# Two layers of windowed attention with relative positions: the token order inside the attention becomes column by column within each pair of image rows

## The reference, cut to what matters

```python
attn = einsum('bqd,bkd->bqk', q * scale, k)
rel_h = einsum('bhwc,hkc->bhwk', qr, Rh)      # table chosen by the query's row h
rel_w = einsum('bhwc,wkc->bhwk', qr, Rw)      # table chosen by the query's column w
attn = attn.reshape(B*nh, H, W, H, W) + rel_h[:, :, :, :, None] + rel_w[:, :, :, None, :]
out = softmax(attn.reshape(B*nh, HW, HW)) @ v
x = x + out @ proj_w.T + proj_b               # once per layer
```

## Time and profile before

| | us |
|---|---|
| median of 3 runs (lowest, highest) | 2332.41 (2329.14, 2334.24) |
| the profiled execution | 2339.97 |
| its span, first to last instruction | 2338.2 |
| TensorE, VectorE, ScalarE, GpSimd busy | 2094.7, 1653.4, 1621.4, 714.4 |
| mean granted TensorE clock in the span | 0.978 of full speed |

### The profile page before, as it was taken

One profiled execution on the slowest core, in us unless ns is written; L12 is line 12 of the kernel. 1 busy time (PEld: TensorE's weight loads), 2 busy tenths in 40 slices (PEclk: granted clock), 3 DMA queues, 4 the chain that ended last, 5 costly groups with the idle time before them and its releaser, 6 DMA issues.

```text
span 2338.2 us, 73485 instructions
## 1 busy us (share of the span) xinstructions
PE 2094.7 (90%) x27904; PEld 1595.9 (68%) x27904; DVE 1653.4 (71%) x3923; ACT 1621.4 (69%) x3713; POOL 714.4 (31%) x1796
## 2 busy tenths in 40 slices
PE   1899999999999989999999999899989999999998
PEld 1677676776767767667667766677766766777765
DVE  5677777667767677777677777677767777777675
ACT  0577777677767667767676777677767776777675
POOL 1233323333333233333233333233223333333230
PEclk9899999999999999999999999999999999999999
DMA  1333434333434333433333443344334343334331
GB/s 47 84 94 95 104 91 105 91 92 91 103 93 97 90 94 93 101 93 93 91 98 91 94 103 96 88 96 100 91 91 102 94 100 93 94 93 103 91 92 47
DMA packets 170550, 216.34 MB, mean 93 GB/s; under 512 B 29783, under 2 KB 138072, under 8 KB 170202
## 3 DMA queue, kind: packets, MB, share of 16 engines
q1 hardware_dynamic: 170202, 211.64, 37.7%
HBM read 117.00 MB, written 57.80 MB: 75 GB/s over the span
## 4 chain that ended last, share of the span: by engine, by line
PE 39%; DMA 33%; SPq 14%; DVE 6%; issue 4%; ACT 3%; POOL 1%; POOLq 0%; ACTq 0%; DVEq 0%
PE ps_m L412 18%; DMA q_st<-mrow 17%; DMA k_dram<-qk_hl 10%; PE ps_sc L538 7%; PE ps_max L525 6%; SPq L375 6%; DMA q_dram<-qk_hl 6%; DVE qk_hl L734 4%; PE ps_o L557 3%; SPq L382 3%; ACT qk_hl L598 2%; SPq L341 2%; SPq L387 2%; PE ps_m L501 2%; DVE rel_hl L776 1%
## 5 line engine op out<-in xcount | busy, mean ns | idle before, releaser
L722 DVE TENSOR_REDUCE mx<-ps_max 98x2 f32<-98x392 f32 x1536 | 819.4, 562 | 232.6 <-PE ps_max L525 215.5
L586 ACT ACTIVATE probs<-ps_sc 98x392 f32<-98x392 f32 x1536 | 714.5, 497 | 232.3 <-PE ps_sc L538 198.2
L525 PE MATMUL ps_max<-k_st,q_st 124*98 124x196 f16 x3072 | 548.9, 261 | 82.4 <-DVE mx L722 82.1
L538 PE MATMUL ps_sc<-q_st,k_st 125*98 125x196 f16 x3072 | 523.3, 252 | 95.6 <-DMA q_st<-mrow 94.1
L776 DVE TENSOR_TENSOR rel_hl<-ps_m,rel_hi 64x504 f16<-64x504 f32 (+1 forms) x768 | 431.4, 562 | 162.0 <-ACT rel_hi L643 152.9
L525 PEld LDWEIGHTS ps_max<-k_st,q_st 124*98 124x98 f16 x3072 | 295.0, 126 | 296.4 <-issue 198.0
L538 PEld LDWEIGHTS ps_sc<-q_st,k_st 125*98 125x98 f16 x3072 | 320.9, 126 | 123.1 <-DMA q_st<-mrow 120.4
L557 PE MATMUL ps_o<-probs,v_st 98*32 98x196 f32 x6144 | 389.6, 340 | 0.5 <-ACT o_sb L578 0.5
L634 ACT ACTIVATE rel_hi<-ps_m,is_lo 64x504 f16<-64x504 f32 (+1 forms) x384 | 223.9, 583 | 189.1 <-PE ps_m L471 185.7
L471 PE MATMUL ps_m<-q_st,rel_st 64*32 64x84 f16 x7168 | 341.6, 266 | 4.8 <-DVE rel_hl L776 4.5
L809 POOL TENSOR_TENSOR msq<-mv 96x2 f32<-96x2 f32 x128 | 24.4, 191 | 1007.1 <-DVE mv L748 1007.1
(11 more groups left out here) (72 smaller groups left out, 3293.8 us busy)
## 6 DMA issues: line engine op xcount, KB each, us to landing
q_st<-q_dram SPq DMA_DIRECT2D x128, 294.0 KB, 3.8
k_st<-k_dram SPq DMA_DIRECT2D x256, 147.0 KB, 3.9
q_dram<-qk_hl SPq DMA_DIRECT2D x128, 147.0 KB, 2.6
k_dram<-qk_hl SPq DMA_DIRECT2D x128, 147.0 KB, 2.7
q_st<-rel_hl SPq DMA_DIRECT2D x256, 73.5 KB
q_st<-rel_hl SPq DMA_DIRECT2D x256, 64.3 KB
xa<-in_x SPq DMA_DIRECT2D x64, 147.0 KB
xd<-in_x SPq DMA_DIRECT2D x64, 147.0 KB
```

Of the source, the lines that this page charges most:

```text
L525: last = nc.tensor.matmul(ps_max[head % 2][0:HT, h * TOK:h * TOK + TOK], q_st[u.r][0:R_MAX, head, h, :], k_st[u.r][0:R_MAX, head, :], star ...
L538: last = nc.tensor.matmul(ps_sc[head % 2][0:HT, kt * TOK:kt * TOK + TOK], k_st[u.r][0:STACK, head, kt * HT:kt * HT + HT], q_st[u.r][0:STAC ...
L586: nc.scalar.activation(probs[head][:, :, :], ps_sc[head % 2][0:HT, 0:2 * TOK].rearrange("p (k t) -> p k t", k=2), ACT.Exp, scale=1.0 / (QS ...
L722: nc.vector.reduce_max(mx[u.r % 2][:, head, :], ps_max[head % 2][0:HT, 0:2 * TOK].rearrange("p (q k) -> p q k", q=2), axis=AX.X).then_inc( ...
```

## The change

Tokens are ordered column by column within each pair of rows: token number = 28 x (row / 2) + 2 x column + (row mod 2), the integer quotient taken. The tokens are put into this order where ScalarE copies `xT` out of PSUM, and put back where it copies `o_sb`. The one-hot rows are put into it once, by a new VectorE copy into `oh_f16`, from which the 48 copies are now made (f16 to f16). In the rel matmuls a row's 14 queries now lie 4 bytes apart and its results 8 bytes apart; a column's queries lie in seven pairs per head, the two of a pair next to each other both in `q_st` and in the bank, the pairs 56 bytes apart in `q_st` and 48 in the bank (16 in `rel2`). The evacuations of a bank keep their number and their sizes; the column ones write runs of 12 elements (4 in `rel2`) instead of 6 (2). No slot, bank, buffer or DMA changes.

```diff
         oh_raw = sb("oh_raw", [128, TOK])
+        oh_f16 = sb("oh_f16", [128, TOK], F16)
...
-            by_col = (dst[64:128, :, :].rearrange("p h (a b) -> p (h a) b", a=SIDE)[:, :, a0:a0 + n],
-                      ps[64:128, 0:n * HH * SIDE].rearrange("p (x b) -> p x b", b=n))
+            by_col = (dst[64:128, :, :].rearrange("p h (k x) -> p (h k) x", k=HALF)[:, :, 2 * a0:2 * (a0 + n)],
+                      ps[64:128, 0:n * HH * SIDE].rearrange("p (x y) -> p x y", y=2 * n))
...
                                 if axis == 0:
-                                    to = to.rearrange("p (h a b) -> p h a b", h=HH, a=rows)[:, :, i, :]
+                                    to = to.rearrange("p (h k b r) -> p h k r b", h=HH, r=2, b=SIDE)[:, :, i // 2, i % 2, :]
+                                    q = q.rearrange("p h (k b r) -> p h k r b", r=2, b=SIDE)[:, :, a // 2, a % 2, :]
                                 else:
-                                    to = to.rearrange("p (x b) -> p x b", b=rows)[:, :, i]
-                                last = nc.tensor.matmul(
-                                    to, rel_st[:, lay, axis, w:w + RW],
-                                    q[:, :, a * SIDE:a * SIDE + SIDE] if axis == 0 else q[:, :, a::SIDE],
-                                    start=True, stop=True)
+                                    to = to.rearrange("p (x b r) -> p x b r", b=rows, r=2)[:, :, i, :]
+                                    q = q.rearrange("p h (k b r) -> p (h k) b r", r=2, b=SIDE)[:, :, a, :]
+                                last = nc.tensor.matmul(to, rel_st[:, lay, axis, w:w + RW], q, start=True, stop=True)
...
-                            nc.scalar.copy(o_sb[u.r % 2][:, g, :], ps_o[:, 0:TOK]).then_inc(s_o, 1)
+                            nc.scalar.copy(o_sb[u.r % 2][:, g, :].rearrange("p (k r b) -> p k r b", r=2, b=SIDE),
+                                           ps_o[:, 0:TOK].rearrange("p (k b r) -> p k r b", r=2, b=SIDE))\
+                              .then_inc(s_o, 1)
...
-                        nc.scalar.copy(xT[u.r % 2][:, :, :],
-                                       ps_m[BANK["xT"]][0:CC, 0:2 * TOK].rearrange("p (c t) -> p c t", c=2))\
+                        nc.scalar.copy(xT[u.r % 2][:, :, :].rearrange("p c (k b r) -> p (c k) b r", r=2, b=SIDE),
+                                       ps_m[BANK["xT"]][0:CC, 0:2 * TOK]
+                                       .rearrange("p (k r b) -> p k b r", r=2, b=SIDE))\
                           .then_inc(s_xT, 1)
...
             dve.wait_ge(s_const, 16 * 8)
+            nc.vector.tensor_copy(oh_f16[R_REL:STACK, :].rearrange("p (k b r) -> p k r b", r=2, b=SIDE),
+                                  oh_raw[R_REL:STACK, :].rearrange("p (k r b) -> p k r b", r=2, b=SIDE)).then_inc(s_oh, 1)
+            dve.wait_ge(s_oh, 1)
             for i in range(UNROLL):
                 for head in range(HEADS):
-                    nc.vector.tensor_copy(k_st[i][R_REL:STACK, head, :], oh_raw[R_REL:STACK, :])
+                    nc.vector.tensor_copy(k_st[i][R_REL:STACK, head, :], oh_f16[R_REL:STACK, :])
```

More of the change, by code:

```diff
@@ L161, in attention_kernel @@
         s_wlo = sem("s_wlo")
+        s_oh = sem("s_oh")
         s_setup = sem("s_setup")
```

## The result

The changed kernel takes 2392.88 us (median of 4 runs, 2390.59 to 2403.28), the kernel before 2330.77 (4 runs, 2325.98 to 2334.24). The ratio is 1.0277, 95% interval 1.0241 to 1.0313: 62 us slower.

What follows compares the result with a forecast made beforehand. It took a ring through the DRAM round trip and second mrow DMA to bound the kernel. Savings of 7 us and a net 41 us from added clock falls made +34, so 2366 us, range 2322 to 2396.

Steps and rivals of the forecast that it cites:

- the likeliest case: Shorter rel bursts lengthen TensorE's wait before head 6, so the clock falls more often; 2345 to 2390, more falls 0.63.
- The picture of the ring: Loop: qk cast, DRAM round trip, second mrow DMA, head 6, next cast; about 11 us outside TensorE, 6.2 on it.
- Column step: One step of column matmuls in a rel burst: from 0.158 us to 0.079 with pairs, half as many separate accesses.
- Burst lengths: Rel matmul bursts on TensorE: rel0 and rel1 lose 0.40 us each, rel2 0.08; first and second from 1.10 to about 0.7.
- The two waits: TensorE's waits for the maxima (takes up rel1's 0.40 us) and before head 6 (0.48 longer; 94 to about 150 us total).
- Falls: Granted clock dropping to its lower level around head 6: 17 units before, 45 forecast, 28 more, from shares by wait length.
- The place of the falls: Falls were forecast around head 6; rel1's 0.40 us was to vanish in the wait for the maxima.
- The price of a fall: Each clock fall around head 6 lengthens TensorE's slots 10 to 3 from 6.22 to 7.80 us, 1.6 us.
- The sum: Gain of 7 us and net loss of 41 from clock falls: +34, put on the median 2332.41, gives 2366.
- no change: Rel bursts stay as long because separate-word writes set their pace; only the start's -2: 2330; within the bound 0.19.
- faster: Shorter bursts without more clock falls before head 6: -7, and -5 more, 2323 to 2326; faster 0.18 in all.
- Slower by more: Column and row matmuls both at row pace: waits grow 0.72 us, 39 more falls, 2384, or 2400 if longer; chance 0.2.

Runs made afterwards that it cites:

- e7: Kernel before, with rel column matmuls reading runs of 14 and writing one run (wrong column terms), for shorter bursts; 2540.34 us, ratio 1.083.
- e1: Changed kernel plus 8 matmuls with overwritten results before head 6's wait for the second mrow DMA; 2342.43 us, ratio 1.0007 to the kernel before.
- e3: Changed kernel with SyncE issuing the second mrow DMA before it waits for q and k's round trip (three slot numbers); 2165.62 us.
- e4: Kernel before, with SyncE issuing the second mrow DMA before it waits for q and k's round trip (three slot numbers); 2199.61 us.
- e8: Changed kernel with the second mrow DMA issued earlier and 8 overwritten matmuls in slot 8, before the wait for the maxima; 2117.89 us.
- e10: Kernel before, with the second mrow DMA issued earlier and 8 overwritten matmuls in slot 8; 2197.58 us, ratio 0.9402.
- e2: Changed kernel plus overwritten matmuls, 8 before head 6's wait and 6 in slot 8 before the wait for the maxima; 2332.78 us, ratio 0.9986.
- e5: Kernel before, with single-element reads in rel0's column matmuls and single-word writes in rel1's, reading and writing kept apart (wrong terms); 2412.29 us, one run.
- e6: Kernel before, with paired reads in rel0's column matmuls and paired writes in rel1's, kept apart (wrong terms); 2545.64 us, one run.

## Why the prediction was right, and where its sizes were off

The direction, the sign's cause and the range (2322 to 2396) held; the time was 2366 against 2392.88, so the loss was 62 us where 34 was said. The time is only 3 us inside the range, and above the 2390 to which the likeliest case alone was said to reach.

The ring of each unit can be cut in two at the first `qk` cast. Means over the 123 units that have both parts, counted from the traces (us; the clock is "low" in a unit where it stood at the lower level for some of TensorE's part):

| | head 6 to `qk` cast (TensorE) | `qk` cast to head 6 (the rest) | units with the clock low in TensorE's part, and that part in them |
|---|---|---|---|
| before | 6.48 | 11.12 | 17, 8.13 |
| changed | 6.94 | 11.13 | 48, 8.06 |
| e7 | 7.49 | 11.39 | 99, 7.80 |
| e1 | 6.32 | 11.32 | 8, 7.95 |

Where the clock stayed, TensorE's part takes 6.21 or 6.22 us in all four. So the loss is in TensorE's part, 56 us over these units, and the rest of the ring has not changed.

- **The picture of the ring**: right. DMA and its issue are still some four tenths of the chain, and e3 and e4 show the ring by opening it. The sign I had named against it, units at full clock shorter by 0.4 us, did not come: head 6 to head 6 takes 17.32 us before and 17.18 after (means of 101 and 65 of these units), and their scatter does not tell 0.14 from nothing.
- **Column step**: 0.079 forecast, 0.076 measured (0.379 us from the first to the last of a burst, a fifth of it). My reason, a cost per separate access, fits the reads of singles and pairs; I allowed row matmuls 0.079 at most, and they pace at 0.067.
- **Burst lengths**: the first mis-sized term. I counted five steps (0.40 us) and 0.08 for rel2, but the last matmul of a burst is shorter as well. 1.10 went to 0.63 and 0.47 to 0.33, together 0.61 us and not 0.48. With the ring open and the clock held, the mean unit is 0.59 us shorter (15.77 in e8, 16.36 in e10).
- **The two waits**: 51 us more for the maxima, as rel1's 0.40 us x 128 = 51 said; 50 us more before head 6, 61 said. The 13 units with a fall in the middle all reach head 6 without a wait.
- **Evacuations, permuted copies**: no change, as taken. **Start**: -2.3 us, -2 said. The 4 us of the units without a wait can't be seen: the rest of the ring is 1 us longer over the 123 units. Such units were miscounted, too: 24 have no wait over 0.15 us, not 13, and 128 less the 105 waits of the earlier trace rows is already 23.
- **Falls**: 45 near head 6 forecast, 35 came, and 13 came in the middle, behind the wait for the maxima. The profile before had none there. That 48 is near 45 is luck in part: two errors meet. Near head 6 the share of long waits with a fall was too high, as it stood on 8 waits: of the 38 waits over 1.6 us in the changed kernel 26 were followed by a fall, where 7 of 8 were before (6 of 21 between 1.2 and 1.6, 3 of 34 between 0.7 and 1.2, none of 34 below).
- **The place of the falls**: the step that is wrong in kind is the one that has rel1's 0.40 us go "into the standstill behind the maxima" at no cost, though that standstill grew from 0.63 to 1.04 us. A fall there can take TensorE's slack and more (21.6 us for the unit above), and all 13 run on into TensorE's part of the next unit, which takes 8.20 us in them. 17 falls hold 72 us at the lower level before, 4.2 us each, and 48 hold 270 after, 5.6 each, because those of the middle are so long.
- **The price of a fall**: 1.6 us forecast, 1.9 before and 1.8 after (8.13 and 8.06 against 6.22). I had priced one fall from the earlier trace rows, 7.80 us; the 17 of the same trace would have given 1.9. e1 says the same: 8 units with the clock low for 48 take 75 us off TensorE's part, 1.9 each, while the rest of the ring grows by 23 us with the fillers.
- **The sum**: the two profiled executions differ by 51 us (2390.59 and 2339.97). Of these the falls make 56 (41 said), the rest of the ring 1, the start and the ends of the pipeline -7. So 17 of the 28 us that are missing in the forecast lie in the terms above. The other 11 are no mechanism: the profiled execution before was 9 us above its median and the one after 2 us below.
- **The mean clock**: 0.95 said, 0.939 measured.
- **The rivals**: no change (bursts as long) fell with the first burst; faster (no more falls) with the clock (its price of -7 and -5 more would be 2320 to 2325, not 2323 to 2326). Slower by more, bursts at the row pace, was priced at 2384 to 2400; e7 has such bursts and took 2540.34, with 76 falls in the middle, for which the sum has no term. At the burst length of the changed kernel that gap was small. The Trainium skill, TensorE: Matmul & The Clock Gate, section "Why this matters for your kernels", warns of idle gaps longer than any wait here. That shorter ones are free does not hold in these runs: filling waits of 1 to 2 us took 50 (e1) and 60 us (e2) off the changed kernel.

What stays open: why one wait is followed by a fall and another of the same length is not. The wait of 1.81 us above passed, while in the kernel before 8 of 30 waits between 1.2 and 1.6 us did not. The counts give a share for each length, not a cause for each fall.

## What to carry to other kernels

Before an engine's work is shortened, find the wait that its stretch ends in: if that wait is set by another ring, the saving becomes a standstill, and on TensorE a standstill of a microsecond can cost more than was saved (here 1.04 us behind the maxima, with 13 falls). Then open the ring first (here three slot numbers in one DMA queue, 6%) and the same edit turns into a gain of 3 to 4% (e10 to e8). Where a short standstill can't be removed, matmuls whose result is overwritten hold the clock; they were worth 60 us in the changed kernel. The best version found, e8, has the change, the new DMA order and the fillers: 2117.89 us, 9% below the kernel before.

## What the runs showed of the hardware that I had not expected

A matmul of 84 f16 columns starts every 0.042 us in its quarter where its moving operand and result lie in runs, 0.068 where each word of the result stands alone, 0.075 where the operand comes in pairs 56 bytes apart, and 0.154 where it comes in single elements 28 bytes apart (e5, e6, e7). With f16 read 4 bytes apart it was 0.049, with results in pairs 48 bytes apart 0.042. The slower of read and write sets the step: with both in single elements it is 0.153, with both in pairs 0.074. The VectorE copies of 61 x 196 from f16 to f16 came every 0.125 us, from f32 every 0.176. ScalarE's copies kept their 323 and 482 ns with every second word, or words 56 bytes apart, read from PSUM.
